# Mixture weights of a Perceiver kernel: turned by a block-permuting load and 32x32 transposes on VectorE instead of on TensorE

## The chip, the core and the metric
One core of one Trainium2 chip runs the whole kernel as one program. The metric is the device time of one execution in microseconds (us); less is better. TensorE does the matrix products (in the profile PE, and PEld for its weight loads), VectorE (DVE) and ScalarE (ACT) the element-wise work, GpSimd (POOL) some small work, and SyncE (SP) issues most DMAs. All four read and write SBUF, 128 partitions wide; TensorE's results go to PSUM, eight banks of 128x512 f32 (`bank`).

## The reference
Two layers over x (16 rows of 64 latents, 512 wide) and a context of 16x512x512: cross attention, gated attention, a quantised product, a second cross attention, a linear attention, and at the end a mixture of experts. The change lies in the mixture and in when its first weights are loaded. What the mixture computes:

```python
logits = einsum('bsd,ed->bse', hidden_states, gate_w) + gate_b
scores = softmax(logits); top_v, top_i = top_k(scores, 2); val_sum = top_v.sum(-1)
for e in range(8):
    gate = (top_i == e).sum(-1) * val_sum
    inter = einsum('bsd,fd->bsf', hidden_states, wi) + bi + (hidden_states @ lora_A[e].T) @ lora_B[e].T
    out = out + gate[..., None] * (relu(inter) @ wo.T + bo)
```

wi is 2048x512 and wo 512x2048. The part with wi and wo is the same for all experts, so the kernel computes it once per hidden column and adds the low-rank part of the two chosen experts.

## The kernel before
`build` runs five stages one behind the other. Each engine has an instruction list of its own, written out by hand, and waits on semaphores (`Signal` for engines, `Landed` for DMAs, 16 per DMA). The fourth stage, `l1_linear_attention`, works on eight pairs of batch rows; its matrix of values lies in XT, pair j in row block j, and the product of pair j with it (line 2232) counts `rows_out`. The fifth stage, `l1_mixture` (line 2420), reuses XT as two buffers of 1 MB, `raw[:, 0]` and `raw[:, 1]`, for the raw weights.

wi and wo are each 16 tiles of 128 hidden columns: tile w = 0 to 15 is of wi, w = 16 to 31 of wo. They come in eight groups of four tiles, q = 0 to 3 of wi and 4 to 7 of wo, each one DMA of 1 MB (`load_half`, line 2488) into `raw[:, q % 2]`. The contraction must lie on the partitions, so each tile is turned: `turn_weight_pe` (line 2525) makes four 128x128 transposes on TensorE into bank 6 or 7, `turn_weight_a` (line 2784) rounds the bank to the high half of a weight, `turn_weight_v` (line 2672) subtracts that from the bank and stores the low half. Every product is three passes (high by high, high by low, low by high), line 289 in `product`.

The stage has three parts on TensorE (`tensor`, line 2607):

- the start: rows of x, logits, lora_B and lora_A are turned and multiplied; VectorE makes softmax, the two largest and their one-hot rows `one` (lines 2714 to 2736), TensorE turns those (line 2643), ScalarE copies them (`oneT`, line 2831), two products pick the experts. Tiles 0 and 1 are turned in between.
- the hidden part: 32 steps u over (f, n), f the hidden tile and n one of two halves of 512 rows. `hidden_pe` makes 12 products with the turned wi tile f, `expert_pe` 3, `second_pe` 3; ScalarE makes one relu (line 2852), VectorE the other and the sum (lines 2760, 2763). Tile f + 1 is turned in step u = 2f, one behind the next; a wi tile lives in one of two buffers `wT`.
- the output part: 32 steps w of 12 products (`produce_pe`), with hidden tile and wo tile f = w % 16 (all 16 stay in `woT`). `split_hidden_a` and `split_hidden_v` round each hidden tile into `hR`, two buffers, in the step before. wo tile w + 1 is turned in step w of the first 16; the other 16 turn nothing.

On SP `load_half(0)` waits for the first transposed rows of the mixture (`turned`), `load_half(1)` for the eighth pair (`rows_out(PAIRS - 1)`), and each later group until the group two before it has been turned (`wt_pe`). The same waits stand in order on SP, ahead of the stores of the output.

Of the kernel before, what the change touches and what calls it, by code (L numbers as in the profile page):

```python
# [7 lines left out]
F32R = mybir.dt.float32r  # L8
# [5 lines left out]
P = 128  # L14
NI, NP, D = 16, 64, 512
# [53 lines left out]
def build(nc, a, out):  # L69
# [3 lines left out]
    def sb(stack, name, shape, dt=F32):  # L73
        return stack.enter_context(nc.sbuf_tensor(name, shape, dt))
# [4 lines left out]
    def landed(name):  # L79
        return Landed(ctx.enter_context(nc.semaphore(name)))  # L80

    with ctx:
# [2337 lines left out]
        def l1_mixture():  # L2420
# [10 lines left out]
            AT = sb(ph, "AT", [P, 2, C, P], F32R)  # L2431
            wT = sb(ph, "wT6", [P, 2, 2, D], F32R)
            hR = sb(ph, "hR", [P, 2, 2, 512], F32R)
# [14 lines left out]
            BT = sb(early, "BT", [P, 2, FF], F32R)  # L2448
            z = sb(early, "z6", [P, 2, 2, ROWS], F32R)
            early.close()  # L2450
            woT = sb(late, "woT", [P, FT, 2, D], F32R)
            acc = (4, 5, 2, 3)
            wide = lambda ap: ap.unsqueeze(2).broadcast_to([P, G, E])
# [4 lines left out]

            half_in = [landed("half_in_0"), landed("half_in_1")]
            spread_a = signal("f_spread")  # L2460
# [25 lines left out]


            def load_half(q):
                dst = raw[:, q % 2, :]
                if q < FT // 4:  # L2490
                    sp.dma_start(dst.rearrange("p (t k) -> p t k", t=4),
                                 a["L1_ffn_wi"].rearrange("(t p) k -> p t k", p=P)[:, 4 * q:4 * q + 4, :]).then_inc(half_in[q % 2].s, 16)
                else:
                    lo = 512 * (q - FT // 4)
                    sp.dma_start(dst.rearrange("p (c f) -> p c f", c=C),
                                 a["L1_ffn_wo"].rearrange("(c p) f -> p c f", p=P)[:, :, lo:lo + 512]).then_inc(half_in[q % 2].s, 16)

            def sync():

                sp.wait_ge(turned.s, turned(5 * G))  # L2500
                load_half(0)
                sp.wait_ge(rows_out.s, rows_out(PAIRS - 1))
                load_half(1)
                for q in range(2, 2 * FT // 4):
                    sp.wait_ge(wt_pe.s, wt_pe(4 * (q - 2) + 3))
                    load_half(q)

            def gpsimd():
# [15 lines left out]

            def turn_weight_pe(w):
                if w < 2:
                    pe.wait_ge(bt_v.s, bt_v(2 + w))
                else:
                    pe.wait_ge(wt_v.s, wt_v(w))
                pe.wait_ge(half_in[(w // 4) % 2].s, half_in[(w // 4) % 2](w // 8))  # L2530
                half = raw[:, (w // 4) % 2, :]
                for k in range(4):
                    src = (half.rearrange("p (t k) -> p t k", t=4)[:, w % 4, k * P:(k + 1) * P] if w < FT else
                           half.rearrange("p (c f) -> p c f", c=C)[:, k, (w % 4) * P:(w % 4 + 1) * P])
                    ins = pe.transpose(bank[:, 6 + w % 2, k * P:(k + 1) * P], src, ident[:])  # L2535
                ins.then_inc(wt_pe.s, 1)

            def hidden_pe(f, n, u):
                cols = slice(n * 512, (n + 1) * 512)
                pe.wait_ge(wt_v.s, wt_v(2 + f))  # L2540
                if u >= 4:
                    pe.wait_ge(relu2.s, relu2(u - 4))
                elif u >= 2:
                    pe.wait_ge(pick_a.s, pick_a(u))
                product(bank[:, hb(u), :], lambda h, c: wT[:, f % 2, h, c * P:(c + 1) * P], lambda h, c: xT[:, h, c, cols], C,
                        last=False)

# [59 lines left out]
            def tensor():  # L2607
# [27 lines left out]
                for n in range(N2):  # L2635
                    cols = slice(n * 512, (n + 1) * 512)
                    product(bank[:, 4 + n, :], lambda h, c: AT[:, h, c, :], lambda h, c: xT[:, h, c, cols], C).then_inc(down.s, 1)
                    if n == 0:
                        turn_weight_pe(0)
                hidden_pe(*tiles[0], 0)  # L2640
# [4 lines left out]
                ins.then_inc(one_pe.s, 1)  # L2645
                turn_weight_pe(1)
                pe.wait_ge(one_a.s, one_a(0))
# [6 lines left out]
                for u in range(len(tiles) + 1):  # L2654
                    if u < len(tiles):
                        if u >= 4:
                            hidden_pe(*tiles[u], u)
                        if u == len(tiles) - 1:
                            turn_weight_pe(FT)
                        expert_pe(*tiles[u], u)  # L2660
                    if u and u % N2 == 0 and u // N2 + 1 < FT:
                        turn_weight_pe(u // N2 + 1)
                    if u:
                        second_pe(*tiles[u - 1], u - 1)
                for w in range(N2 * FT + 1):
                    if 0 < w < FT:
                        turn_weight_pe(FT + w)
# [20 lines left out]
            def lora_b_v(q):  # L2688
                cols = slice(q * 512, (q + 1) * 512)
                dve.wait_ge(bt_a.s, bt_a(q))  # L2690
                split_v(BT[:, 1, cols], bank[:, bt_at[q % 2], :], BT[:, 0, cols]).then_inc(bt_v.s, 1)

            def vector():
# [15 lines left out]
                for q in range(2):  # L2709
                    lora_b_v(q)  # L2710
                dve.wait_ge(lg_pe.s, lg_pe(1))
                dve.wait_ge(row_in.s, row_in(1))
# [5 lines left out]
                for q in range(2, 4):  # L2718
                    lora_b_v(q)
                turn_weight_v(0)  # L2720
                dve.wait_ge(gate_a.s, gate_a(0))
# [14 lines left out]
                ins.then_inc(one_v.s, 1)  # L2736
                turn_weight_v(1)
                dve.wait_ge(down.s, down(1))
# [29 lines left out]
                for w in range(N2 * FT + 1):  # L2768
                    if w < N2 * FT:
                        if 0 < w < FT:  # L2770
                            turn_weight_v(FT + w)
                        if w:
                            split_hidden_v(w)
                    if w and (w - 1) % FT == FT - 1:
                        n = (w - 1) // FT
                        for g in range(4):
                            xg = X[:, 4 * n + g, :]
                            dve.wait_ge(prod.s, prod(n * (FT + 3) + FT - 1 + g))
                            dve.wait_ge(biased.s, biased(G - 1))
                            dve.scalar_tensor_tensor(out=xg, in0=bank[:, acc[g], :], scalar=m1[:, 4 * n + g:4 * n + g + 1],  # L2780
                                                     in1=xg, op0=ALU.mult, op1=ALU.add).then_inc(xsum.s, 1)


            def turn_weight_a(w):
                act.wait_ge(wt_pe.s, wt_pe(w))
                if 2 <= w < FT:
                    act.wait_ge(hid_pe.s, hid_pe(N2 * (w - 2) + N2 - 1))
                at = wT[:, w % 2, :, :] if w < FT else woT[:, w - FT, :, :]
                split_a(at[:, 0, :], bank[:, 6 + w % 2, :]).then_inc(wt_a.s, 1)

# [16 lines left out]
            def scalar():  # L2807
# [15 lines left out]
                act.wait_ge(lg_pe.s, lg_pe(0))  # L2823
                act.copy(lgT, bank[0:E, 4:6, :]).then_inc(lg_a.s, 1)
                for q in range(2, 4):
                    lora_b_a(q)
                turn_weight_a(0)
# [4 lines left out]
                turn_weight_a(1)  # L2832
                for n in range(N2):
# [88 lines left out]
```

## Time and profile before

| what | us |
|---|---|
| median of 3 runs | 1252.72 |
| shortest and longest run | 1250.03, 1260.43 |
| span of the profiled execution, first to last instruction | 1248.6 |
| the hidden part from its third step to its last product with wi | 1013.4 to 1144.6 |
| the output part | 1147.7 to 1242.2 |

The profile gives no time of the profiled execution other than its span; the shortest run is 1.4 us and the median 4.1 us longer than that span. All times in the rows are from the start of the span. The busy time of TensorE is modelled: products follow each other in less than the busy time of one, so the distance from one group to the next in the chain says what a group costs.

### The profile page before, as it was taken

To read this page: it belongs to the slowest core of one execution; us is meant where nothing else is said; L and a number is where in the kernel's file an instruction comes from. 1 tells how busy PE (TensorE), PEld (TensorE's weight loads), DVE (VectorE), ACT (ScalarE), POOL (GpSimd) and SP (SyncE) were. 2 spreads that over 40 slices of the span, in tenths; PEclk is the share of its full clock that TensorE was granted. 3 is DMA by queue.
4 is the path that set the end of the run, shared out by engine and by line. 5 is a ranking of instruction groups with operands and counts; after the bars stand their busy time and mean duration, and the time that the engine had idled before them with its cause. 6 is when DMAs were issued, how large, how long until landed. Compare 5 with 4: busy or idle time off the path is not lost.

```text
span 1248.6 us, 25643 instructions
## 1 busy us (share of the span) xinstructions
PE 1202.0 (96%) x10969; PEld 895.9 (72%) x10969; DVE 708.9 (57%) x1569; ACT 520.2 (42%) x1028; POOL 141.5 (11%) x164
## 2 busy tenths in 40 slices
PE   7999889999999999999999999999899999999997
PEld 5654478766466777777777777777787678888886
DVE  5456486767783555555555555555686755434432
ACT  3344447742132554545444444445453332222321
POOL 1300031166523000000000000000131100000000
PEclk9999999999999999999999999999999999999999
DMA  9669500201113110000010011110500201111210
GB/s 357 255 234 407 200 1 1 76 1 41 62 55 131 51 54 35 35 35 35 35 35 35 35 44 38 57 37 2 86 1 1 77 1 34 34 35 34 68 34 34
DMA packets 48485, 88.21 MB, mean 71 GB/s; under 512 B 19002, under 2 KB 20076, under 8 KB 44148
## 3 DMA queue, kind: packets, MB, share of 16 engines
q1 hardware_dynamic: 47024, 85.48, 19.4%
q8 instruction: 87, 1.43, 0.5%
q10 hardware_dynamic: 1348, 1.09, 0.4%
q14 instruction: 26, 0.21, 0.1%
HBM read 65.59 MB, written 20.97 MB: 69 GB/s over the span
## 4 chain that ended last, share of the span: by engine, by line
PE 88%; DVE 6%; ACT 3%; issue 1%; POOL 1%; DMA 1%; POOLq 0%; SPq 0%; DVEq 0%; ACTq 0%
PE bank L289 59%; PE bank L245 4%; PE bank L1790 3%; PE bank L1811 2%; PE bank L559 2%; PE bank L577 2%; PE bank L1138 2%; PE bank L1117 2%; PE bank L235 1%; DVE W L1380 1%; PE bank L495 1%; PE bank L2535 1%; PE bank L1086 1%; PE bank L1070 1%; PE bank L1094 1%
## 5 line engine op out<-in xcount | busy, mean ns | idle before, releaser
L2023 ACT ACTIVATE W<-W,low 128x512 f32<-128x512 f32 x128 | 90.9, 713 | 57.2 <-DVE low L1929 57.2
L2003 ACT ACTIVATE K<-bank,vecT 128x512 f32<-128x512 f32 x64 | 43.8, 689 | 167.0 <-PE bank L289 167.0
L225 POOL TENSOR_TENSOR rstd<-rstd,half_pow 128x1 f32<-128x1 f32 x48 | 30.9, 645 | 684.0 <-DVE rstd L221 684.0
L1902 DVE TENSOR_TENSOR W<-bank,vecT 128x256 f32<-128x256 f32 x16 | 6.8, 425 | 164.2 <-PE bank L1811 164.2
L1929 DVE CUSTOM_DVE_ANT_0 W<-bank,W 128x512 f32<-128x512 f32 x128 | 80.8, 687 | 30.6 <-PE bank L1790 30.6
L289 PE MATMUL bank<-xT,wT 128*128 128x512 f32 x384 | 92.8, 391 | 0.8 <-ACT W L2837 0.5
L289 PE MATMUL bank<-ctxT,Wkv 128*128 128x512 f32 x384 | 93.5, 396 | 0.0
L289 PE MATMUL bank<-Wq,Wkv 128*128 128x512 f32 x384 | 93.0, 394 | 0.0
L289 PE MATMUL bank<-Wkv,ctxT 128*128 128x512 f32 x384 | 92.9, 394 | 0.0
L289 PE MATMUL bank<-Wkv,Wq 128*128 128x512 f32 x384 | 92.1, 395 | 0.0
L289 PE MATMUL bank<-woT,hR 128*128 128x512 f32 x384 | 91.7, 394 | 0.1
L289 PEld LDWEIGHTS bank<-Wkv,ctxT 128*128 128x128 f32 x384 | 70.8, 188 | 27.1 <-issue 13.0
L289 PEld LDWEIGHTS bank<-Wkv,Wq 128*128 128x128 f32 x384 | 70.8, 188 | 26.8 <-issue 12.6
L289 PEld LDWEIGHTS bank<-xT,wT 128*128 128x128 f32 x384 | 71.9, 188 | 17.3 <-issue 1.3
L289 PEld LDWEIGHTS bank<-ctxT,Wkv 128*128 128x128 f32 x384 | 70.8, 188 | 15.2 <-issue 0.5
L289 PEld LDWEIGHTS bank<-woT,hR 128*128 128x128 f32 x384 | 70.9, 188 | 14.9 <-DVE W_late L2763 0.5
L289 PEld LDWEIGHTS bank<-Wq,Wkv 128*128 128x128 f32 x384 | 70.8, 188 | 14.8
L2030 ACT COPY PT<-bank 128x512 f32<-128x512 f32 x128 | 65.8, 600 | 19.4 <-PE bank L245 19.4
L1937 DVE TENSOR_SCALAR W<-W,total 128x512 f32<-128x512 f32 x128 | 62.3, 487 | 4.6
L2852 ACT ACTIVATE h<-bank,vecT 128x512 f32<-128x512 f32 x32 | 22.1, 690 | 95.2 <-PE bank L289 90.9
L245 PEld LDWEIGHTS bank<-ident,W 32*128 32x128 f32 x2752 | 46.3, 137 | 19.2 <-issue 11.5
L289 PE MATMUL bank<-z,BT 128*128 128x512 f32 x192 | 53.0, 400 | 0.1
(343 smaller groups left out, 2171.4 us busy)
## 6 DMA issues: line engine op xcount, KB each, us to landing
W<-ctx_turned SPq DMA_DIRECT2D x16, 1024.0 KB, 4.8
W<-in_ctx_dram SPq DMA_DIRECT2D x8, 1024.0 KB, 10.6
ctx_turned<-ctxT SPq DMA_DIRECT2D x8, 1024.0 KB, 7.6
ctx_turned<-W SPq DMA_DIRECT2D x8, 1024.0 KB, 6.6
XT<-in_ctx_dram SPq DMA_DIRECT2D x4, 1024.0 KB, 11.7
XT<-in_L_ffn_wi_dram SPq DMA_DIRECT2D x4, 1024.0 KB, 5.9
XT<-in_L_ffn_wo_dram SPq DMA_DIRECT2D x4, 1024.0 KB, 5.1
raw_own<-in_ctx_dram SPq DMA_DIRECT2D x3, 1024.0 KB, 10.7
```

The lines of the kernel that those rows point to most:

```text
L225: pool.tensor_tensor(rstd[:, g:g + 1], rstd[:, g:g + 1], half_pow[:], ALU.pow).then_inc(rstd_ok.s, 1)
L245: ins = pe.transpose(bank[:, first + r, to:to + 32], src_of(t, k)[strip, :], ident[strip, strip])
L289: ins = pe.matmul(dst, stationary(x, k), moving(y, k), start=(first and n == 0), stop=(last and n == len(passes) - 1), skip_group_check=True)
L559: ins = pe.matmul(bank[b * NP:(b + 1) * NP, 4, :], q2T[:, c, j * P + b * NP:j * P + (b + 1) * NP], ctxT[j % 2][:, b, c, :], start=(c == 0) ...
L577: ins = pe.matmul(bank[b * NP:(b + 1) * NP, 6, :], pT[:, k, b * NP:(b + 1) * NP], raws[j % 4][:, b, k, :], start=(k == 0), stop=(k == KT - 1))
L1117: ins = pe.matmul(bank[:, 7, :], y[:, g % 3, c * P:(c + 1) * P], slot(7)[:, c, :], start=(c == 0), stop=(c == C - 1))
L1790: ins = pe.matmul(bank[s2 * NP:(s2 + 1) * NP, 4 + r, :], qT[strip, 2 * rnd + s2, i * NP:(i + 1) * NP], K[strip, 2 * rnd + s2, :], start=Tr ...
L1929: dve.tensor_tensor_reduce(out=PR[:, j, :], in0=bank[:, 4 + j % 4, :], in1=mask, scale=1.0, scalar=3.0e38, op0=ALU.add, op1=ALU.min, accum ...
L1937: dve.tensor_scalar(PR[:, j, :], PR[:, j, :], total[:, j:j + 1], None, ALU.mult).then_inc(probs.s, 1)
L2003: act.activation(K[:, m, :], bank[:, n % 4, :], ACT.Identity, bias=pcol("L1_xattn_bk", m)).then_inc(ring_a.s, 1)
L2023: act.activation(PR[:, j, :], PR[:, j, :], ACT.Exp, bias=low[:, j:j + 1], scale=-1.0, accum_out=total[:, j:j + 1]).then_inc(expd.s, 1)
L2030: act.copy(PT[:, 4 * half:4 * half + 4, :, strip].rearrange("p t k n -> p (t k) n"), bank[:, 4 + n % 4, :].rearrange("p (a n) -> p a n", n ...
```

## The change
TensorE no longer turns wi and wo. Each group of four tiles is loaded by 16 DMAs of 64 KB instead of one of 1 MB. Each takes 32 columns of the weight for one run of 512 rows, and puts them on 32 partitions, 16 blocks of 32 elements side by side: the 32x32 blocks already stand where the turned tile wants them, and only inside each block are rows and columns still the wrong way round. VectorE's 32x32 transpose (`blocks_of`, four instructions of 128x512 per group, in place) does that. ScalarE and VectorE then split the tile from SBUF instead of from a bank.

- Group 0 is loaded when the fourth pair has used the values (`rows_out(3)`) instead of in the mixture.
- Groups 2 to 5 wait for VectorE's split of the group two before (`wt_v`). Group 6, the third of wo, has a buffer of its own, `spare_half`, in space that x and the wi tiles held, and waits for the last product with wi (`hid_last`). Group 7 waits for the split of tile 19.
- `blocks_of` of group q + 1 stands behind the split of tiles 4q + 1 and 4q + 2, two each; for groups 5 to 7 one instruction stands behind each of the output part's steps 0 to 11. All of them stand in VectorE's one list.
- Tile 0 is split before the gate's softmax, tile 1 before the two largest are sought. The buffers `wT` now lie in space that `woT` takes over, so ScalarE's first write to `woT` waits for `hid_last`.

```diff
 def load_half(q):
-    dst = raw[:, q % 2, :]
...
+    landing, half, _ = homes[q]
+    for r in range(4):
+        rows = slice(32 * r, 32 * r + 32)
+        for k in range(4):
+            if q < FT // 4:
+                src = a["L1_ffn_wi"][512 * q:512 * q + 512, k * P:(k + 1) * P]
+            else:
+                lo = 512 * (q - FT // 4) + k * P
+                src = a["L1_ffn_wo"][:, lo:lo + P]
+            sp.dma_start(half[rows, k * 512:(k + 1) * 512].rearrange("p (t n) -> p t n", n=32),
+                         src[:, rows].rearrange("(t p) n -> p t n", p=32)).then_inc(landing.s, 16)
...
+def blocks_of(q, k):
+    if k == 0:
+        half_landed(dve, q)
+    part = homes[q][1][:, k * 512:(k + 1) * 512]
+    dve.transpose(part, part).then_inc(blocks_v.s, 1)
 def turn_weight_v(w):
...
-    split_v(at[:, 1, :], bank[:, 6 + w % 2, :], at[:, 0, :]).then_inc(wt_v.s, 1)
+    split_v(at[:, 1, :].rearrange("p (c k) -> p c k", c=C), weight(w),
+            at[:, 0, :].rearrange("p (c k) -> p c k", c=C)).then_inc(wt_v.s, 1)
+    q = w // 4 + 1
+    if w < FT and w % 4 in (1, 2):
+        for k in range(2):
+            blocks_of(q, 2 * (w % 4 - 1) + k)
...
 (output part, VectorE)
                         split_hidden_v(w)
+                    if w < FT - 4:
+                        blocks_of(FT // 4 + 1 + w // 4, w % 4)
```

TensorE, the end of the hidden part and the start of the output part (`XT` is the raw weight, `hR` the split hidden tile). Before:

```order
 L289 MATMUL bank<-xT,wT 128x512 x12
 L2535 MATMUL bank<-ident,XT 128x128 x4
 L289 MATMUL bank<-z,BT 128x512 x9
 L2535 MATMUL bank<-ident,XT 128x128 x4
 L289 MATMUL bank<-woT,hR 128x512 x12
 L2535 MATMUL bank<-ident,XT 128x128 x4
 L289 MATMUL bank<-woT,hR 128x512 x12
```

The same place of the change:

```order
 L289 MATMUL bank<-z,BT 128x512 x6
 L289 MATMUL bank<-xT,wT 128x512 x12
 L289 MATMUL bank<-z,BT 128x512 x9
 L289 MATMUL bank<-woT,hR 128x512 x384
```

The transposes have left the list, and all 384 products of the output part follow one another.

VectorE in the mixture's start, from the split of lora_B (`BT`) on. Before:

```order
 L306 TENSOR_TENSOR BT<-bank,BT 128x512 [waits f_bt_a] x2
 L2714 TENSOR_TENSOR S<-bank,gb 128x64 [waits setup_pool,row_in,f_lg_pe]
 L2716 TENSOR_REDUCE m<-S 128x8 [waits dve_seq]
 L2717 TENSOR_TENSOR S<-S,m 128x64 [waits dve_seq]
 L306 TENSOR_TENSOR BT<-bank,BT 128x512 [waits f_bt_a] x2
 L306 TENSOR_TENSOR wT<-bank,wT 128x512 [waits wt_a]
 L2722 TENSOR_REDUCE m<-S 128x8 [waits f_gate_a]
```

The same place of the change:

```order
 L306 TENSOR_TENSOR BT<-bank,BT 128x512 [waits f_bt_a] x2
 L2681 STREAM_TRANSPOSE XT<-XT 128x512 [waits half_in_0]
 L2681 STREAM_TRANSPOSE XT<-XT 128x512 x3
 L306 TENSOR_TENSOR wT<-XT,wT 128x512 [waits wt_a]
 L2733 TENSOR_TENSOR S<-bank,gb 128x64 [waits setup_pool,row_in,f_lg_pe]
 L2735 TENSOR_REDUCE m<-S 128x8 [waits dve_seq]
 L2736 TENSOR_TENSOR S<-S,m 128x64 [waits dve_seq]
 L306 TENSOR_TENSOR BT<-bank,BT 128x512 [waits f_bt_a] x2
 L306 TENSOR_TENSOR wT<-XT,wT 128x512 [waits wt_a]
 L2681 STREAM_TRANSPOSE XT<-XT 128x512 [waits half_in_1]
 L2681 STREAM_TRANSPOSE XT<-XT 128x512
 L2741 TENSOR_REDUCE m<-S 128x8 [waits f_gate_a]
```

Group 0's four transposes, the split of tile 1 and the first two transposes of group 1 have come ahead of the search for the two largest (from line 2741 on), and with them the waits for both groups' landing.

SP, the last loads (line 2506 is `load_half`). Before:

```order
 L2495 DMA XT<-in_L_ffn_wo_dram 128x4x512 [waits wt_pe] x4
 L2863 DMA out_dram<-X 8x8x512 [waits xsum] x12
```

The same place of the change, the last three of the four wo groups:

```order
 L2506 DMA XT<-in_L_ffn_wo_dram 32x16x32 [waits wt_v]
 L2506 DMA XT<-in_L_ffn_wo_dram 32x16x32 x15
 L2506 DMA spare_half<-in_L_ffn_wo_dram 32x16x32 [waits f_hid_last]
 L2506 DMA spare_half<-in_L_ffn_wo_dram 32x16x32 x15
 L2506 DMA XT<-in_L_ffn_wo_dram 32x16x32 [waits wt_v]
 L2506 DMA XT<-in_L_ffn_wo_dram 32x16x32 x15
 L2886 DMA out_dram<-X 8x8x512 [waits xsum] x12
```

Each of the groups is 16 issues where it was one, and the engines that they wait for are VectorE and, for group 6, TensorE.

## Rows read from the trace of the kernel before

**Rows 1.** The page: busy time, share of the span and instructions of TensorE and VectorE.
```profile
PE 1202.0 (96%) x10969; PEld 895.9 (72%) x10969; DVE 708.9 (57%) x1569; ACT 520.2 (42%) x1028; POOL 141.5 (11%) x164
```

**Rows 2.** The chain that ended last, in order of time: start us, us, what.
```profile
1006.56 0.89 PE bank L2643 x8
...
1025.18 3.70 PE bank L289 x15
1028.87 0.44 PE bank L2535 x4
1029.31 8.19 PE bank L289 x36
...
1132.59 0.44 PE bank L2535 x4
...
1144.62 0.44 PE bank L2535 x4
...
1149.41 1.65 PE bank L289 x6
1151.06 0.44 PE bank L2535 x4
...
1192.71 0.44 PE bank L2535 x4
1193.15 49.03 PE bank L289 x216
```

**Rows 3.** Groups by line, all of the mixture: busy us, mean ns of one.
```profile
L2535 PE MATMUL bank<-ident,XT 128*128 128x128 f32 x128 | 19.1, 272 | 0.0
```

**Rows 4.** The order of time in the mixture's start: start us, us, engine, line, operation.
```profile
992.49 1.28 DVE L306 TENSOR_TENSOR BT<-bank,BT 128x512 fp32r<-128x512 f32 x2
...
995.99 1.00 ACT L2824 COPY W<-bank 8x1024 f32<-8x1024 f32 x1 [4.57 <-PE bank L289]
...
1002.36 0.21 DVE L2722 TENSOR_REDUCE m<-S 128x8 f32<-128x64 f32 x1
...
1007.27 0.60 PE L2535 MATMUL bank<-ident,XT 128*128 128x128 f32 x4
1007.47 1.00 ACT L2831 CAST oneT<-bank 16x1024 fp32r<-16x1024 f32 x1 [5.60 <-PE bank L2643]
```

**Rows 5.** The order of time at the start of the output part.
```profile
1148.66 0.69 DVE L2763 TENSOR_TENSOR W_late<-W_late,h 128x512 f32<-128x512 f32 x1
```

**Rows 6.** Groups by line on VectorE in the mixture and just before: busy us, mean ns.
```profile
L2760 DVE TENSOR_SCALAR W<-bank,vecT 128x512 f32<-128x512 f32 x28 | 20.9, 746 | 23.4 <-PE bank L289 23.4
L2763 DVE TENSOR_TENSOR W<-W,h 128x512 f32<-128x512 f32 x28 | 19.4, 692 | 1.0
L306 DVE TENSOR_TENSOR woT<-bank,woT 128x512 fp32r<-128x512 f32 x16 | 11.1, 691 | 28.2 <-ACT woT L297 28.2
L2766 DVE SCALAR_TENSOR_TENSOR X<-bo,m,X 128x512 f32<-128x512 f32 x8 | 6.0, 744 | 0.0
L2338 DVE TENSOR_SCALAR q<-q,low 128x512 f32<-128x512 f32 x8 | 3.9, 487 | 0.3
L2283 DVE TENSOR_TENSOR W<-W,ext 128x512 f32<-128x512 f32 x4 | 3.4, 850 | 0.1
```

**Rows 7.** The order of time: products of the fourth and the eighth pair.
```profile
965.23 1.02 PE L2232 MATMUL bank<-XT,at 128*128 128x512 f32 x2
...
981.91 1.02 PE L2232 MATMUL bank<-XT,at 128*128 128x512 f32 x2
```

**Rows 8.** SP's issues by line: ns min/median/max, first and last start us.
```profile
L1731 SPq DMA_DIRECT2D X<-x_rows x8: 333/437/451, 378.6 to 381.8; - x8
L2125 SPq DMA_DIRECT2D W<-in_L_ffn_lora_A_dram x1: 1357/1357/1357, 876.2 to 876.2; - x1
```

**Rows 9.** DMA issues, the line of lora_B: KB each, median us from issue to landing.
```profile
W<-in_L_ffn_lora_B_dram SPq DMA_DIRECT2D x8, 128.0 KB, 4.3
```

**Rows 10.** DMA packets from 888 to 894 us, while lora_B lands in runs of 64 bytes.
```profile
DMA packets 9931, 0.63 MB, mean 105 GB/s; under 512 B 9931, under 2 KB 9931, under 8 KB 9931
```

More of the change, by code:

```diff
@@ L2431, in l1_mixture @@
             AT = sb(ph, "AT", [P, 2, C, P], F32R)
-            wT = sb(ph, "wT6", [P, 2, 2, D], F32R)
             hR = sb(ph, "hR", [P, 2, 2, 512], F32R)
@@ L2449, in l1_mixture @@
             z = sb(early, "z6", [P, 2, 2, ROWS], F32R)
+            wT = sb(early, "wT6", [P, 2, 2, D], F32R)
             early.close()
             woT = sb(late, "woT", [P, FT, 2, D], F32R)
+            spare_half = sb(late, "spare_half", [P, 4 * D])
             acc = (4, 5, 2, 3)
@@ L2457, in l1_mixture @@
             gw_src = bank[:, 4, 0:C * E].rearrange("k (c e) -> k c e", c=C)
-            half_in = [landed("half_in_0"), landed("half_in_1")]
+            half_in = [landed("half_in_0"), landed("half_in_1"), landed("half_in_2")]
+            blocks_v = signal("f_blocks_v")
+            hid_last = signal("f_hid_last")
             spread_a = signal("f_spread")
@@ L2485, in produced, with half_landed, weight @@
                 return prod(n * (FT + 3) + (f if f < FT - 1 else FT + 2))
+            homes = [(half_in[2], spare_half[:], 0) if q == 6 else
+                     (half_in[(q - q // 7) % 2], raw[:, (q - q // 7) % 2, :], (q - q // 7) // 2)
+                     for q in range(2 * FT // 4)]
             def load_half(q):
-                dst = raw[:, q % 2, :]
[L2490 to L2496, printed above, removed]
+                landing, half, _ = homes[q]
[9 more added lines that the diff above has]
+                                     src[:, rows].rearrange("(t p) n -> p t n", p=32)).then_inc(landing.s, 16)
+            def half_landed(engine, q):
+                landing, _, n = homes[q]
+                engine.wait_ge(landing.s, landing(16 * n + 15))
+            def weight(w):
+                half = homes[w // 4][1]
+                if w < FT:
+                    return half.rearrange("p (c t k) -> p t c k", c=C, t=4)[:, w % 4, :, :]
+                return half[:, (w % 4) * 512:(w % 4 + 1) * 512].rearrange("p (c k) -> p c k", c=C)
             def sync():
-                sp.wait_ge(turned.s, turned(5 * G))
+                sp.wait_ge(rows_out.s, rows_out(3))
                 load_half(0)
@@ L2503, in sync @@
                 load_half(1)
-                for q in range(2, 2 * FT // 4):
-                    sp.wait_ge(wt_pe.s, wt_pe(4 * (q - 2) + 3))
+                for q in range(2, 6):
+                    sp.wait_ge(wt_v.s, wt_v(2 + 4 * (q - 2) + 3))
                     load_half(q)
+                sp.wait_ge(hid_last.s, hid_last(0))
+                load_half(6)
+                sp.wait_ge(wt_v.s, wt_v(2 + FT + 3))
+                load_half(7)
             def gpsimd():
@@ L2522, in gpsimd @@
                 ins.then_inc(setup_pool.s, 1)
[L2525 to L2536, printed above, removed]
             def hidden_pe(f, n, u):
@@ L2544, in hidden_pe @@
                     pe.wait_ge(pick_a.s, pick_a(u))
-                product(bank[:, hb(u), :], lambda h, c: wT[:, f % 2, h, c * P:(c + 1) * P], lambda h, c: xT[:, h, c, cols], C,
-                        last=False)
+                return product(bank[:, hb(u), :], lambda h, c: wT[:, f % 2, h, c * P:(c + 1) * P], lambda h, c: xT[:, h, c, cols], C,
+                               last=False)
             def expert_pe(f, n, u):
@@ L2637, in tensor @@
                     product(bank[:, 4 + n, :], lambda h, c: AT[:, h, c, :], lambda h, c: xT[:, h, c, cols], C).then_inc(down.s, 1)
-                    if n == 0:
-                        turn_weight_pe(0)
                 hidden_pe(*tiles[0], 0)
@@ L2645, in tensor @@
                 ins.then_inc(one_pe.s, 1)
-                turn_weight_pe(1)
                 pe.wait_ge(one_a.s, one_a(0))
@@ L2656, in tensor @@
                         if u >= 4:
-                            hidden_pe(*tiles[u], u)
-                        if u == len(tiles) - 1:
-                            turn_weight_pe(FT)
+                            ins = hidden_pe(*tiles[u], u)
+                            if u == len(tiles) - 1:
+                                ins.then_inc(hid_last.s, 1)
                         expert_pe(*tiles[u], u)
-                    if u and u % N2 == 0 and u // N2 + 1 < FT:
-                        turn_weight_pe(u // N2 + 1)
                     if u:
@@ L2665, in tensor @@
                 for w in range(N2 * FT + 1):
-                    if 0 < w < FT:
-                        turn_weight_pe(FT + w)
                     if w:
                         produce_pe(w - 1)
+            def blocks_of(q, k):
[3 more added lines that the diff above has]
+                dve.transpose(part, part).then_inc(blocks_v.s, 1)
             def turn_weight_v(w):
@@ L2710, in vector @@
                     lora_b_v(q)
+                for k in range(4):
+                    blocks_of(0, k)
+                turn_weight_v(0)
                 dve.wait_ge(lg_pe.s, lg_pe(1))
@@ L2719, in vector @@
                     lora_b_v(q)
-                turn_weight_v(0)
+                turn_weight_v(1)
                 dve.wait_ge(gate_a.s, gate_a(0))
@@ L2736, in vector @@
                 ins.then_inc(one_v.s, 1)
-                turn_weight_v(1)
                 dve.wait_ge(down.s, down(1))
@@ L2784, in turn_weight_a @@
             def turn_weight_a(w):
-                act.wait_ge(wt_pe.s, wt_pe(w))
+                q = w // 4
+                act.wait_ge(blocks_v.s, blocks_v(4 * q + (3 if w < FT else w % 4)))
                 if 2 <= w < FT:
                     act.wait_ge(hid_pe.s, hid_pe(N2 * (w - 2) + N2 - 1))
+                if w == FT:
+                    act.wait_ge(hid_last.s, hid_last(0))
                 at = wT[:, w % 2, :, :] if w < FT else woT[:, w - FT, :, :]
-                split_a(at[:, 0, :], bank[:, 6 + w % 2, :]).then_inc(wt_a.s, 1)
+                split_a(at[:, 0, :].rearrange("p (c k) -> p c k", c=C), weight(w)).then_inc(wt_a.s, 1)
             def split_hidden_a(w):
@@ L2824, in scalar @@
                 act.copy(lgT, bank[0:E, 4:6, :]).then_inc(lg_a.s, 1)
+                turn_weight_a(0)
                 for q in range(2, 4):
                     lora_b_a(q)
-                turn_weight_a(0)
+                turn_weight_a(1)
                 act.wait_ge(gate_v.s, gate_v(0))
@@ L2831, in scalar @@
                 act.copy(oneT[:], bank[0:2 * E, 0:2, :].rearrange("e b n -> e (b n)")).then_inc(one_a.s, 1)
-                turn_weight_a(1)
                 for n in range(N2):
```

## The prediction

> **What bounds the kernel now.** I read the page's busy shares first: TensorE is busy 96% of the span, VectorE 57% [rows 1]. In most places, then, the end moves only if something leaves TensorE's list or TensorE waits. Next the chain in order of time: through the mixture it is TensorE nearly everywhere, and between its products stand the groups of four transposes of a weight tile, 0.44 us each [rows 2]. The group of line 2535 counts 128 of them with 19.1 us of busy time, 272 ns each [rows 3]. That sum overstates them, since busy spans of neighbours overlap; the reader is to take the distance between steps of the chain instead.
>
> **What is removed.** One product costs 49.03 / 216 = 0.227 us where nothing stands between [rows 2]. A tile of the hidden part takes (1132.59 - 1028.87) / 12 = 8.64 us for 36 products and one group of transposes [rows 2]; 36 products are 8.17, so a group costs 0.47 us. A step of the output part takes (1192.71 - 1151.06) / 13 = 3.20 us [rows 2], its 12 products 2.72, so a group costs 0.48 us. Not each of the 32 groups lies on the path:
>
> - Tile 0's group ends in the products before the one-hot rows at 1006.56 [rows 2], so TensorE gets there 0.44 us earlier, if those rows are ready. I count 0.2 (below).
> - Tile 1's group ran at 1007.27 while TensorE waited for ScalarE's oneT, which ended at 1008.47 [rows 4]: 0.
> - Tile 2's split was itself awaited: the chain reaches TensorE only at 1025.18 [rows 2]. The relu and sum that hold it are unchanged: 0.
> - Tiles 3 to 15: 13 x 0.47 = 6.1 us. Tile 16 at 1144.62 [rows 2]: 0.44 us.
> - Tile 17's group lay in a wait too: TensorE needs the last hidden sum, which VectorE starts at 1148.66 and ends at 1149.35 [rows 5], and goes on at 1149.41 [rows 2]: 0.
> - Tiles 18 to 31: 14 x 0.48 = 6.7 us.
>
> Together 13.4 us. If all 32 groups counted it would be 32 x 0.48 = 15.4 us; this is the most that the change can give.
>
> **What VectorE gets.** 32 transposes of 128x512 f32, an operation that the trace does not show. The nearest rows on 128x512 f32 go from 0.487 us (a scale in SBUF) to 0.850 us [rows 6]; I take 0.69, what the plain two-operand operation on these shapes takes [rows 6], since a transpose also handles each element once and nothing says that it gets the scale's speed. The Trainium skill, "Vector Engine (DVE) Microarchitecture Reference", section "The reshape front-end and per-opcode configuration", says that the transpose sustains one element per cycle per lane; with the 0.96 GHz of "VectorE: DVE Perf Modes", section "Specifications", that is 0.53 us (an estimate from the two pages), and by it tile 0's group would give its whole 0.44 us and the sum would grow by 0.2 us. No run here shows that figure.
>
> In the hidden part VectorE has per tile two relus of 0.746, two sums of 0.692, one split of 0.69, for the first eight steps a bias of 0.744 each, and now at most two transposes: 2.88 + 0.69 + 1.49 + 1.38 = 6.4 us of the tile's 8.17 [rows 6]. In the output part it has 0.69 (split of the tile) + 0.69 (split of the hidden tile) + 0.69 = 2.1 of 2.72 us. It is hidden in both, as long as one transpose takes less than 2.72 - 1.38 = 1.34 us. The cover is thinner at two places:
>
> - The start. VectorE ends the lora_B splits at 993.8 [rows 4]. Four transposes take it to 996.5; ScalarE is not free before 997.0, when its copy of the logits ends [rows 4], so they cost nothing. Tile 0's rounding and split end at 998.3, three small gate operations 0.7 us later, two lora_B splits at 1000.4, tile 1's split at 1001.0, two transposes at 1002.4. There the search for the two largest begins, which began at 1002.36 before [rows 4]: no later, but hardly earlier either, hence 0.2 of 0.44 us. With the ends 0.487 and 0.850 the start moves by 0.4 us down or 0.7 up.
> - The first output step. Behind the last sum VectorE now makes one transpose, the split of tile 17 and that of hidden tile 1: 1149.35 + 3 x 0.65, about 1.95 us later. TensorE, free 1.65 us after 1149.41 [rows 2], waits some 0.2 us.
>
> ScalarE and VectorE read the tile from SBUF instead of a bank; the nearest rows differ by a few hundredths and both have room. So 0.2 + 6.1 + 0.44 + 6.7 - 0.2 = 13.2 us.
>
> **What SP gets.** 16 issues for each group instead of one; 8192 packets of 128 bytes instead of 512 of 2 KB. Issues: 0.437 us for a median one of eight in a row, which begin 0.46 us apart [rows 8], so 16 take 7.4 us; the last lands 4.3 us later as lora_B's did [rows 9]: 11.7 us. Packets: 9931 of 64 bytes went in 6 us at 105 GB/s [rows 10]. A packet of 128 bytes costs at least one and at most two of those, so the group takes 5 to 10 us, beside the issues. I take 12 us. From above: the dearest single issue of a small load is 1.357 us [rows 8], and 16 of those with 4.3 us are 26 us.
>
> What waits for it is VectorE's list, with everything behind it, from these moments on:
>
> - Group 0: issued when the fourth pair is done, 966.3, wanted at 993.8 [rows 4, 7]: 27 us of cover.
> - Group 1: issued at 982.9 [rows 7], wanted at 1001.0 on the path of the start: 18 us.
> - Groups 2 to 4: issued at the split of tile 4q - 5, wanted four half-tile steps of 4.1 us later, 16.3 us; TensorE feels it some 4 us later still, since VectorE's relus are needed two steps on: 20 us.
> - Group 5: from the split of tile 15 to the last hidden sum, 15 us.
> - Group 6: from the last product with wi, 1144.6, to VectorE's step 4, J + 3 x 2.72 with J = 1149.4, about 13 us, with 2 us of slack, since hidden tiles are split ahead: 15 us.
> - Group 7: five steps of 2.72 us and the same slack: 15.6 us.
>
> At 12 us all are covered. SP's queue holds nothing that is due: the stores come after the last group. Earlier loading of group 0 only moves a transfer to where SP is idle.
>
> The span was 1248.6 us; less 13.2 it is 1235.4. The page gives no other time of that execution. The median of the runs shown is 4.1 us and the shortest 1.4 us above the span; against the median, 1252.7 - 13.2 = 1239.5 us.
>
> **The rivals.**
>
> *The loads land late.* One mechanism: SP needs more than about 1 us per issue, because small packets back up. For it: the 1.357 us issue; packets at one quarter of the size of anything loaded from so wide-pitched rows here. Against it: the issues 0.46 us apart and the packet rate. The price by the covers above: at 20.6 us per group, group 1 costs 2.6, groups 2 to 4 together 1.8, group 5 5.6, which gives group 6 its time, and group 7 5.0: 15, and the gain is gone. At 23 us it is 5 + 9 + 8 + 7 = 29, so about 16 slower (1268); at 26 us 8 + 18 + 11 + 10 = 47, so 1286. The Trainium skill speaks for this rival: "SBUF — State Buffer", section "The DMA setup-cost knee", gives every DMA a nearly fixed cost of some 2 us and advises the largest single transfer; sixteen that paid it one after the other would take 32 us (an estimate from that page), and the kernel would be far slower. The page also says that the cost is mostly the wait for completion, and rows 8 show eight issues inside 3.7 us, so I expect most of it to overlap.
>
> *Transposes twice as dear.* At 1.4 us each the four of group 0 end 2.4 us after ScalarE is free, the two of group 1 add 1.4, and each of twelve output steps gets 0.1 us longer: 5 us lost, 1244.5. For it: nothing but that the operation is not in the trace.
>
> *Less is given back.* TensorE's steps shrink less than by a whole group, because another wait stands right behind. In the output part the rounding and splitting of the next hidden tile but one needs 1.3 us of a step of 2.72, so I see none; half the gain would be 1246.
>
> **How the numbers follow.** Forecast 0.72, 1239.5 us, by itself 1236 to 1243: the most that 15.4 us of gain allow on one side, the dearer transpose and the spread of the runs on the other. Late loads 0.18: a third of it between 1243 and 1265, the rest above. Dear transposes 0.06, less given back 0.04. The range goes from 1235 (15.4 us below the span, with the shortest run's 1.4 us) to 1266 (loads of some 22.5 us), which leaves out about 0.12 above. About 1%, 12.5 us, is what a measurement of this kernel can tell from no change. The forecast lies just beyond it, at 13.2: of its 0.72 I give 0.46 to faster and 0.26 to the same; the rivals give the same 0.14 and slower 0.14.
>
> **What would show it.** Right: no line 2535; output steps of 2.72 us from the first to the last; hidden tiles of 8.17 us; VectorE transposes near 0.69 us; no DMA as a releaser of VectorE; the search for the two largest at about 1002. Wrong: VectorE waiting for a raw weight's DMA in front of a transpose, SP issues near or above 1 us, or TensorE waiting for `hR` or relu behind such a wait.

## The result, and the profile after

The changed kernel takes 1239.51 us (median of 4 runs, 1236.52 to 1242.36), the kernel before, run beside it, 1254.68. The ratio is 0.988, with a 95% interval of 0.9856 to 0.9905: faster by 1.2%. Six more runs on another occasion gave 0.9899 (0.9863 to 0.9935). The forecast was 1239.5 us.

The page of the changed kernel: busy time, share of the span and instructions.

```profile
PE 1192.2 (96%) x10841; PEld 884.5 (71%) x10841; DVE 727.4 (59%) x1601; ACT 520.7 (42%) x1028; POOL 141.3 (11%) x164
...
DMA packets 111845, 88.21 MB, mean 71 GB/s; under 512 B 86458, under 2 KB 87532, under 8 KB 107508
```

Against [rows 1] TensorE has lost the 128 transposes and 10 us of busy time; VectorE has gained 32 instructions and 18.5 us.

The span of this execution is only 7.5 us shorter than that of before (1241.1 and 1248.6), and that is not the change's doing: it reached the first product of line 2232, ahead of the mixture, 7.2 us late (957.31 for 950.12; an execution of the kernel before without turning, below, reached it at 962.07). Two stretches of the granted clock of TensorE (the last column but two), of the changed kernel:

```profile
120.00:160.00 40.00, 36.51 (x292) 18.70 (x289) 17.95 (x36) 17.94 (x39) 0.55 (x1) 0.96 0.61 224
...
880.00:920.00 40.00, 36.28 (x361) 30.27 (x355) 25.75 (x48) 17.84 (x33) 6.84 (x10) 0.88 0.40 67
```

The kernel before has 1.00 in both, for the same work. So the spans of two executions are not to be compared; the parts of the mixture are. The yardstick below runs from the first product of line 2232 to VectorE's addition that waits for TensorE's last product: 292.08 us before (950.12 to 1242.20), 277.29 us after (957.31 to 1234.60). Of the 14.79 us of difference, 1.32 is a stretch in the start of before's mixture in which the granted clock was at its lower level, 1.2 GHz (eight transposes of line 235 took 1.97 us there and 1.25 after, the eight behind them 1.54 and 0.87, the next eight 0.87 and 0.94). That leaves 13.47 us; the forecast was 13.2. The chain of before there, the same place of the changed kernel, and a stretch of the granted clock of before:

```profile
986.03 1.97 PE bank L235 x8
988.00 1.54 PE bank L2599 x8
989.54 0.87 PE bank L235 x8
```

```profile
993.22 1.25 PE bank L235 x8
994.47 0.87 PE bank L2611 x8
995.35 0.94 PE bank L235 x8
```

```profile
986.00:988.00 2.00, 1.97 (x9) 1.97 (x10) 2.00 (x5) 0.59 (x1) 1.40 (x6) 0.50 0.84 274
```

The chain that ended last of the changed kernel, in order of time:

```profile
1011.96 0.89 PE bank L2653 x8
...
1030.60 113.24 PE bank L289 x498
...
1147.40 0.69 DVE W_late L2781
1148.09 0.62 DVE XT L2681
1148.71 0.57 DVE woT L306
1149.29 0.61 DVE hR L306
...
1149.94 84.63 PE bank L289 x372
1234.60 0.75 DVE X L2800
```

Where [rows 2] had a row of four transposes after every 36 and every 12 products, there is now one row for 498 products and one for 372, at 0.227 us each. From tile 2's split to the last product with wi it was 1025.18 to 1144.62, 119.44 us, and is 113.24: 6.20 less. From the second output step to the last product it was 91.12 us (41.65 + 49.47, from 1151.06) and is 84.63: 6.49 less. The passage between the two parts gave 0.34, and the start 0.46.

What was added, on VectorE and SP (ns min/median/max, first and last start), with the time to landing:

```profile
L2681 DVE STREAM_TRANSPOSE XT<-XT x28: 669/703/706, 999.6 to 1176.1; 128x512 f32<-128x512 f32 x28
L2681 DVE STREAM_TRANSPOSE spare_half<-spare_half x4: 704/704/706, 1157.0 to 1165.2; 128x512 f32<-128x512 f32 x4
```

```profile
L2506 SPq DMA_DIRECT2D XT<-in_L_ffn_wi_dram x64: 311/488/1578, 973.5 to 1076.8; - x64
L2506 SPq DMA_DIRECT2D XT<-in_L_ffn_wo_dram x48: 311/488/1714, 1101.6 to 1160.7; - x48
L2506 SPq DMA_DIRECT2D spare_half<-in_L_ffn_wo_dram x16: 487/488/497, 1143.9 to 1151.9; - x16
...
DMA to landing us min/median/max: 1.8/2.1/3.3
```

One transpose takes 0.703 us alone, and in a row they begin 0.59 to 0.63 us apart. An issue takes 0.488 us and lands 2.1 us after it began (4.3 for lora_B, [rows 9]). From its first issue to its last landing a group takes 9.8 to 10.1 us, and groups 0 and 5, in which one issue takes 1.6 and 1.7 us, 11.2. No wait of VectorE in the mixture ends with a DMA. What is left between a group's landing and VectorE's first transpose of it is 5 to 15 us, but only 2.5 and 3.0 for groups 5 and 6.

VectorE and ScalarE in the mixture's start, in order of time:

```profile
999.61 2.49 DVE L2681 STREAM_TRANSPOSE XT<-XT 128x512 f32<-128x512 f32 x4
...
1001.86 1.00 ACT L2847 COPY W<-bank 8x1024 f32<-8x1024 f32 x1 [4.56 <-PE bank L289]
...
1006.47 1.30 DVE L2681 STREAM_TRANSPOSE XT<-XT 128x512 f32<-128x512 f32 x2
1007.69 0.18 DVE L2741 TENSOR_REDUCE m<-S 128x8 f32<-128x64 f32 x1
```

### The profile page after: what moved, and what is told of

Same layout as the page of the kernel before. It is cut to its first block, busy times and chain, and to the rows that moved or that the text cites. A ratio compares the mean times of both kernels' runs of the same rounds, so it can differ in the third digit from the quotient of the medians.

```text
span 1241.1 us, 25508 instructions
## 1 busy us (share of the span) xinstructions
PE 1192.2 (96%) x10841; PEld 884.5 (71%) x10841; DVE 727.4 (59%) x1601; ACT 520.7 (42%) x1028; POOL 141.3 (11%) x164
## 4 chain that ended last, share of the span: by engine, by line
PE 87%; DVE 6%; ACT 3%; DMA 1%; issue 1%; POOL 1%; SPq 0%; POOLq 0%; DVEq 0%; ACTq 0%
PE bank L289 58%; PE bank L245 4%; PE bank L1790 3%; PE bank L559 2%; PE bank L577 2%; PE bank L1811 2%; PE bank L1138 2%; PE bank L1117 2%; DVE W L1380 1%; PE bank L495 1%; PE bank L235 1%; DMA W<-ctx_turned 1%; PE bank L1086 1%; PE bank L1070 1%; PE bank L1094 1%
## 5 line engine op out<-in xcount | busy, mean ns | idle before, releaser
L289 PE MATMUL bank<-woT,hR 128*128 128x512 f32 x384 | 87.8, 390 | 0.7 <-DVE W_late L2781 0.5
L245 PE MATMUL bank<-ident,W 32*128 32x32 f32 x2752 | 51.4, 224 | 2.1 <-DVE W L1937 1.1
```

The lines of the kernel that those rows point to most:

```text
L245: ins = pe.transpose(bank[:, first + r, to:to + 32], src_of(t, k)[strip, :], ident[strip, strip])
```

## The experiments

The theory: the gain is what TensorE's groups of four took where they lay on the path, and VectorE's transposes and SP's small loads are covered but for some tenths. The rivals: they take back part of the gain unseen; or the covers are not where the prediction puts them. Results on the yardstick:

| kernel | us | against the changed one |
|---|---|---|
| before | 292.08 | +14.79 (13.47 at full clock) |
| changed / once more | 277.29 / 277.28 | 0 / -0.01 |
| before without turning | 276.99 | -0.30 |
| three transposes for one | 307.54 | +30.25 |
| group 6 without own buffer | 286.77 | +9.48 |
| group 0 loaded late | 280.66 | +3.37 |
| late, group 1's transposes behind the search | 277.25 | -0.04 |
| 32 / 64 DMAs per group | 297.23 / 420.46 | +19.94 / +143 |
| output transposes a step later | 276.82 | -0.47 |
| the same, with an earlier rounding | 277.61 | +0.32 (-1.03 at full clock) |

The expectations count up to the end of the span, which lies 6.5 to 7.3 us behind the yardstick's end, by when the last stores finish; some count from the fourth pair, 15.1 us later.

**The changed kernel once more.** No edit.

> The changed kernel once more, as the yardstick of the three that run beside it. Both theories: ratio to the kernel before 0.986 to 0.991; from the start of the first product of line 2232 to the end of the span 283.8 us (in the kernel before 298.5), with the same waits in the first output step.

Ratio 0.9899, and 277.28 us: two executions of one kernel agree within 0.01 us on the yardstick. To the end of the span it was 284.6, 0.8 above the expectation; all of that lies behind the last product.

**What turning alone was worth.** The kernel before; nothing turns the weights. The waits for these transposes become waits for the loads, for VectorE's splits and, at the first wo tile, for the last product with wi.

```diff
 def turn_weight_pe(w):
...
-    for k in range(4):
...
-        ins = pe.transpose(bank[:, 6 + w % 2, k * P:(k + 1) * P], src, ident[:])
-    ins.then_inc(wt_pe.s, 1)
+    return
```

> The kernel before with the 128 weight transposes of TensorE (line 2535) left out and nothing in their place: the weight tiles are rounded and split from whatever the banks hold, so the turning of the weights is the part of the computation that is left out. The loads, their two large DMAs apiece and VectorE's work stay as they were. From the start of the fourth pair's product (line 2232) to the end of the span the kernel before needs 283.4 us (1.3 of them a stretch at half the clock), the changed one 268.7. Theory (the whole gain is TensorE's groups, and VectorE's transposes and the small DMAs cost nothing beside 0.4 us in the first output step): 268.0 to 269.0, ratio to the kernel before about 0.989. Rival (VectorE's transposes or the small DMAs take back part of the gain somewhere): under 267.5.

268.5 us from the fourth pair; ratio 0.9912 (0.9886 to 0.9939). With the large loads and without transposes on any engine the kernel is 0.30 us shorter than the changed one. So the new work costs 0.30 us net, and all else that TensorE gave up was gained. The chain of this run:

```profile
1035.51 113.19 PE bank L289 x498
...
1153.00 86.04 PE bank L289 x378
```

It reaches the last product with wi 0.10 us later than the changed kernel and gains 0.40 us behind it; the next run shows where.

**Transposes a step later in the output part.**

```diff
-if w < FT - 4:
-    blocks_of(FT // 4 + 1 + w // 4, w % 4)
+if 0 < w <= FT - 4:
+    blocks_of(FT // 4 + 1 + (w - 1) // 4, (w - 1) % 4)
```

> The changed kernel with VectorE's transposes of the output part one step later, so that none stands between the last hidden sum and the splits of the second output step. Theory (the transpose of 0.62 us there makes TensorE wait 0.43 us in the first output step and nowhere else): 283.4 us from the first product of line 2232 to the end, the wait for hR gone. Rival (the wait is the split of the weight tile, not the transpose in front of it): 283.8 us, the wait still there.

0.47 us shorter. The chain goes straight from the last sum into all later products:

```profile
1146.02 0.70 DVE W_late L2781
...
1146.77 86.01 PE bank L289 x378
```

The wait for `hR` is gone, so the transpose at 1148.09 above was its cause.

**Three transposes for one.**

```diff
 part = homes[q][1][:, k * 512:(k + 1) * 512]
+v(dve.transpose(part, part))
+v(dve.transpose(part, part))
 dve.transpose(part, part).then_inc(blocks_v.s, 1)
```

> The changed kernel with each of VectorE's 128x512 transposes made three times (an odd number, so the block ends as it should). Each further one costs about 0.65 us. Theory (the covers as forecast: thin at the start and in the first output step, 1.34 us per transpose in an output step, wide in the hidden part): start + 7 us (four blocks of group 0 with 8 further transposes, 5.2, and two of group 1 with 4, 2.6, less some slack), output steps 2.1 + 1.3 = 3.4 us for 2.72 in 11 of them, + 5 to 7, hidden part under + 1: from the fourth pair to the end 268.7 + 13 = 280 to 284 us. Rival (VectorE has room everywhere): under 274 us.

298.9 us, 15 above the expected range. By parts: the start +13.3 (7 expected), the hidden part +9.1 (under 1), the rest +7.8 (5 to 7). VectorE in one hidden tile of this run, in order of time:

```profile
1065.38 0.69 DVE L306 TENSOR_TENSOR wT<-XT,wT 128x512 fp32r<-128x512 f32 x1 [2.49 <-ACT wT L297]
1065.98 0.70 DVE L2681 STREAM_TRANSPOSE XT<-XT 128x512 f32<-128x512 f32 x1
...
1069.55 0.71 DVE L2683 STREAM_TRANSPOSE XT<-XT 128x512 f32<-128x512 f32 x1
1070.19 0.71 DVE L2780 TENSOR_SCALAR W<-bank,vecT 128x512 f32<-128x512 f32 x1
...
1075.00 0.69 DVE L306 TENSOR_TENSOR wT<-XT,wT 128x512 fp32r<-128x512 f32 x1 [0.66 <-ACT wT L297]
```

From split to split it is 9.62 us where a tile has 8.17. Six transposes, 4.2 us, stand in one piece ahead of the relu, and ScalarE's relu two steps on waits for VectorE's sum (`h1` has two buffers); TensorE waits for that relu, 5.8 us in all. What makes up the other 3.3 us isn't settled; the granted clock was 0.91 from 1040 to 1060. The expectation had spread the extra work over all tiles; it falls on two of four. Of the start's 13.3 us, 1.45 is a stretch of half clock at line 235 as in before, and 8.3 the later search. The rest is clock: TensorE, after 7.5 us of waiting for the one-hot rows, went on at half of it:

```profile
1012.00:1016.00 4.00, 0.00 (x0) 0.00 (x0) 3.55 (x15) 0.00 (x0) 0.00 (x0) 0.59 0.00 0
1016.00:1020.00 4.00, 1.96 (x9) 1.01 (x9) 0.79 (x4) 1.00 (x1) 0.00 (x0) 0.50 0.00 0
1020.00:1024.00 4.00, 4.00 (x9) 2.77 (x10) 2.07 (x3) 1.07 (x2) 0.00 (x0) 0.50 0.00 0
```

Behind the wait the eight one-hot transposes took 1.89 us for 0.89, and the 12 products 5.40 for 2.95.

**Group 0 loaded late**, as late as in the kernel before:

```diff
-sp.wait_ge(rows_out.s, rows_out(3))
+sp.wait_ge(turned.s, turned(5 * G))
 load_half(0)
```

> The changed kernel with group 0 loaded as late as in the kernel before (when the last pair's tiles are turned, some 20 us later than now) and group 1 still behind the last rows. Theory (a group takes SP 8.3 us of issues and 2 of landing, so both land within a microsecond of the time that VectorE wants them): from the fourth pair to the end 268.7 + 0 to 1 us. Rival (the earlier load of group 0 is what keeps the start covered): + 3 us or more, with a DMA as the releaser of VectorE's first transposes.

The rival holds: +3.37 us. SP issued 32 DMAs in a row, from 988.00 for 18.26 us, so group 1 landed at 1007.9. VectorE, in order of time, and three stretches with TensorE's granted clock:

```profile
1005.44 0.68 DVE L306 TENSOR_TENSOR wT<-XT,wT 128x512 fp32r<-128x512 f32 x1
1007.92 1.31 DVE L2681 STREAM_TRANSPOSE XT<-XT 128x512 f32<-128x512 f32 x2 [1.80 <-DMA XT<-in_L_ffn_wi_dram]
```

```profile
1008.00:1012.00 4.00, 3.52 (x16) 2.59 (x14) 3.62 (x14) 0.00 (x0) 0.00 (x0) 1.00 0.00 0
1012.00:1016.00 4.00, 1.79 (x11) 1.02 (x11) 0.93 (x5) 1.21 (x2) 0.00 (x0) 1.00 0.00 0
1016.00:1020.00 4.00, 4.00 (x11) 3.15 (x12) 2.06 (x3) 0.86 (x2) 0.00 (x0) 0.57 0.00 0
```

A wait of 1.80 us for a DMA, and behind it 1.6 us of half clock: 12 products took 4.54 us for 2.95. The changed kernel at this place:

```profile
1016.00:1020.00 4.00, 3.47 (x15) 2.31 (x14) 1.57 (x3) 1.94 (x4) 0.00 (x0) 1.00 0.00 0
```

**Late, with group 1's first two transposes behind the search.**

```diff
 ins.then_inc(one_v.s, 1)
+for k in range(2):
+    blocks_of(1, k)
 dve.wait_ge(down.s, down(1))
```

(The same two are left out behind tile 1's split.)

> The kernel with the late first group (+3.6 us: 287.4 from the first product of line 2232 to the end), and the two transposes of group 1 that stood ahead of the search for the two largest put behind it, into VectorE's wait of 3.5 us. Theory (the loss came from the place of these two in VectorE's queue, 1.85 us of waiting and 1.6 us of half clock behind it): 283.8 us within 0.5, no stretch at half the clock at 1016 to 1020. Rival (the 16 late transfers disturb something else): 286 us or more.

277.25 us, and 1.00 in every one of these stretches. The late load costs nothing when group 1's two transposes are not in front of work that TensorE waits for.

**Group 6 without a buffer of its own.**

```diff
-for q in range(2, 6):
+for q in range(2, 8):
     sp.wait_ge(wt_v.s, wt_v(2 + 4 * (q - 2) + 3))
     load_half(q)
-sp.wait_ge(hid_last.s, hid_last(0))
-load_half(6)
...
```

> The changed kernel with the first wo group in one of the two old buffers: groups 6 and 7 wait for the split of the last tile of the group two before (tiles 11 and 15 as 4q - 5), as groups 2 to 5 do, and spare_half is not used. That means the group of the third wo quarter no longer begins with the last product with wi but behind the split of the second tile of wo's first group's end. Theory (10.2 us per group must fit in four output steps of 2.72 us, with no slack left): the load of 10.2 us, then a transpose, a rounding and a split of 0.7 each, 12.3 us for 10.9 us of steps less 2 us of run-ahead that is used once; + 2 to + 9 us on 268.7 us, and VectorE's transpose is released by a DMA in the list of waits. Rival (the buffer does nothing, the loads have time anyway): 268.7 within 0.7, and no DMA releases VectorE.

+9.48 us, a little above the range. Two loads are late, by VectorE's waits:

```profile
1160.13 0.71 DVE L2675 STREAM_TRANSPOSE XT<-XT 128x512 f32<-128x512 f32 x1 [5.72 <-DMA XT<-in_L_ffn_wo_dram]
...
1175.04 0.71 DVE L2675 STREAM_TRANSPOSE XT<-XT 128x512 f32<-128x512 f32 x1 [4.17 <-DMA XT<-in_L_ffn_wo_dram]
```

**32 and 64 DMAs per group**, of 32 and 16 KB, the same packets of 128 bytes.

```diff
+for j in range(PARTS):
+    lo_t, n_t = j * (16 // PARTS), 16 // PARTS
...
```

(PARTS is 2 and 4; each DMA loads its share of the 16 blocks.)

> The changed kernel with each group loaded by 32 DMAs of 32 KB instead of 16 of 64 KB, the same 8192 packets of 128 bytes. Theory (an issue takes 0.49 us however little it carries, 0.53 from one to the next): 17 us of issues and 2 of landing, 19 us per group, beyond the cover of groups 1, 5, 6 and 7 as the run without the own buffer and the one with the late first group showed it: 6 to 14 us longer than 283.8 us from the first product of line 2232 to the end, VectorE released by DMAs. Rival (an issue costs by its packets): half the time per issue, 10 us per group as now, 283.8 us.

> The changed kernel with each group loaded by 64 DMAs of 16 KB. Theory (0.49 us per issue however small): 36 us per group, eight of them 288 us in the 230 us from the fourth pair to the last group's use: 80 to 130 us longer. Rival (an issue costs by its packets): under 5 us longer.

The issues and VectorE's waits of the first of the two:

```profile
L2510 SPq DMA_DIRECT2D XT<-in_L_ffn_wi_dram x128: 311/451/1683, 973.3 to 1091.0; - x128
```

```profile
DVE XT L2685 <- DMA XT<-in_L_ffn_wo_dram: 11.3, 3, 5.1
...
DVE XT L2685 <- DMA XT<-in_L_ffn_wi_dram: 7.3, 3, 3.1
...
DVE spare_half L2685 <- DMA spare_half<-in_L_ffn_wo_dram: 5.5, 1, 5.5
```

An issue of half the size takes 0.451 us for 0.488, and of a quarter 0.432: a group's time goes by its DMAs, not its packets. The theory holds, but at 17.2 to 19.1 us per group (19 expected) the price is 19.94 us, not 6 to 14: seven of eight groups are late, by 24.1 us in all. By parts it is 5.05 us in the start, 0.71 in the hidden part and 14.18 behind it. TensorE's longest wait in sum, and three stretches behind its waits:

```profile
PE bank L289 <- DVE hR L306: 10.8, 3, 4.3
```

```profile
1016.00:1020.00 4.00, 4.00 (x10) 2.67 (x10) 2.07 (x3) 1.07 (x2) 0.00 (x0) 0.50 0.00 0
...
1160.00:1164.00 4.00, 4.00 (x13) 3.19 (x14) 2.66 (x5) 0.00 (x0) 0.00 (x0) 0.67 0.43 67
...
1176.00:1180.00 4.00, 4.00 (x12) 3.09 (x11) 2.64 (x5) 0.00 (x0) 0.00 (x0) 0.57 0.44 67
```

So the waits are paid again in clock: in the start group 1 was late by 2.0 us, and the other 3.1 are mostly products at half clock (12 took 5.42 us for 2.95). Behind the hidden part it is some 3 us more, an estimate from the last two stretches.

With 64 DMAs the issues of one group alone take 30 to 33 us, VectorE waits for every group, and the kernel is 143 us longer, above the 130 expected.

**A version with less waiting left.** The kernel with transposes a step later, and ScalarE's rounding of the next wi tile moved ahead of its relu:

```diff
 for u in range(len(tiles) + 1):
+    if u and u % N2 == 0 and u // N2 + 1 < FT:
+        turn_weight_a(u // N2 + 1)
     if u < len(tiles):
...
-    if u and u % N2 == 0 and u // N2 + 1 < FT:
-        turn_weight_a(u // N2 + 1)
```

> The kernel of the run before, and ScalarE's rounding of a hidden part's weight tile put ahead of the relu that it stood behind (it no longer waits for a bank of TensorE's). Theory: tile 2's split begins about 1.3 us earlier, of which TensorE, which stands still for 0.6 us in front of it, gets 0.6: together 282.8 us from the first product of line 2232 to the end, ratio to the kernel before 0.0008 below the changed kernel's. Rival (the relu that now comes 0.6 us later is awaited instead): 283.4 us or more.

Ratio to before 0.989 (0.986 to 0.9919), the changed kernel beside it 0.9899: the runs can't tell them apart. In the profiled execution the clock fell in the start, as it had in the kernel before (1.97 us for the eight transposes of line 235, 1.57 and 0.87 for the next two eights, for 1.25, 0.87 and 0.94): 1.35 us. Without it the yardstick is 276.26, 1.03 less than the changed kernel, as expected; TensorE's wait for tile 2's split is gone from the list of waits. That it beats the changed kernel is shown in the parts of one trace only, with 1.35 us taken off for the clock.

## Why the prediction was right

By its own steps, which add up to 13.5 us for 13.2:

- *Tiles 3 to 15, 6.1 us*: 6.20. *Tiles 18 to 31, 6.7 us*: 6.49. Reading a group's price from the distance between steps of the chain (0.47 and 0.48) instead of its busy time was right: by the busy time of [rows 3] these 27 groups would have been 16.1 us, and 12.69 came.
- *Tile 0, 0.2 of 0.44 us*: all 0.44 came (the start gave 0.46). The search for the two largest began some 0.5 us earlier than before, not "no later, but hardly earlier either". The step that was off is that VectorE's instructions were added up by their durations, while in a row they follow each other faster. From the end of ScalarE's copy to the search 5.4 us were counted and 4.83 came: the rounding and split 1.16 for 1.3, two lora_B splits 1.20 for 1.4, two transposes 1.22 for 1.4. Group 0's four transposes, 2.49 us for 2.7, cost nothing, as forecast: they ended 0.8 us before that copy did. The Trainium skill, "Vector Engine (DVE) Microarchitecture Reference", section "The reshape front-end and per-opcode configuration", led to an estimate of 0.53 us with the clock of "VectorE: DVE Perf Modes", section "Specifications". The trace lies above it, with 0.703 us alone and 0.59 to 0.63 in a row, and its consequence, the whole 0.44 us, came nevertheless.
- *Tiles 1, 2 and 17, nothing; tile 16, 0.44*: the passage from the hidden to the output part gave 0.34, tile 16 less the first output step.
- *First output step, 0.2 us lost*: the splits of the second step ended at 1149.89, and TensorE waited 0.4; the run with later transposes gave 0.47 back.
- *Loads, 12 us per group*: 9.8 to 11.2, and no wait. The issues took a little longer (8.3 us for 7.4, in most groups); landing was 2.1 us, not lora_B's 4.3. The Trainium skill, "SBUF — State Buffer", section "The DMA setup-cost knee", with some 2 us per DMA, agrees with the 2.1 us from issue to landing, but these overlap: 16 DMAs took 9.8 to 11.2 us, not the 32 of the estimate.

That the median came out at 1239.51 is in part luck. Medians of the same kernel on other occasions differ by more than the small errors above: 1243.65 for the changed kernel, and 1252.72, 1254.68 and 1255.22 for the kernel before.

What the prediction had wrong, without harm to its number, is the price of its rivals. *Late loads* was to break even at 20.6 us per group. In the run with 32 DMAs a group took 18.4 us (median), for which the covers of the prediction give 6.6 us (group 1 0.4, group 5 3.4, group 7 2.8), and 19.94 were lost. Three steps failed there:

- The covers of groups 6 and 7 were counted from their own waits, as if SP were free then. SP's queue is one: group 6 began only at 1156.40, when group 5's last issue was out, 7 us after the last product with wi, and group 7 right behind group 6. VectorE waited 5.5 and 5.1 us for them.
- The covers of groups 1 and 5 are shorter than counted: in the changed kernel it is 16.3 us for 18 and 13.8 for 15.
- The sum has no term for the clock behind a wait, some 6 of the 19.94 us by the estimate above.

What held is that TensorE feels a group that is late in the hidden part "some 4 us later still": groups 2 to 4 made VectorE wait 3.1, 2.2 and 2.2 us there, and the hidden part grew by only 0.71.

*Transposes twice as dear* was priced at 5 us with the hidden part free; three for one show that it isn't free where four more transposes come in one piece; twice as dear was not run. And "earlier loading of group 0 only moves a transfer to where SP is idle" missed that this is what frees SP for group 1: the cover of 18 us counted for group 1 holds only so.

## What to carry to other kernels

Price an instruction on a full engine by the distance between steps of the chain, and count it only where no other wait lies in its shadow. When one large DMA becomes many, count issues: from 64 to 16 KB they cost nearly the same here, they queue on one engine, and the cover of each group must be counted from when that queue is free. Work given to an idle engine is hidden step by step, not on the average: ask what stands behind it in that engine's list and put it where that engine waits anyway.

## What the chip showed that was not expected

- A short wait of TensorE cost nearly as much again in clock. With group 0 late it stood still for 1.6 us for the one-hot rows and 1.1 for `oneT`, with eight transposes in between; then the granted clock was 0.57 in 1016 to 1020 and the same products took 1.6 us more. With 32 DMAs, after 1.8 and 1.1 us, it was 0.50. In the changed kernel, with only the 1.1 us, it stayed at 1.00.
- The eight transposes of line 235 in the mixture's start, for which TensorE waits 1.7 us, ran at 1.2 GHz in four of the twelve profiled executions (before, three transposes, 64 DMAs, the last version) and at 2.4 GHz in the others, in code that was the same. With what follows they cost 1.3 to 1.5 us more; part of the spread between runs is there.
- DMAs of 64, 32 and 16 KB cost SP 0.488, 0.451 and 0.432 us to issue.
